# A GRU recurrence on one core: its loop written out, its gates in pair scans, its products placed anew

## The reference

```
hw = h @ gru_w_hh.T                     # 1024 -> 3 x 1024
xr, xz, xn = split(x_t @ gru_w_ih.T);  hr, hz, hn = split(hw)
r = sigmoid(xr + hr);  z = sigmoid(xz + hz)
n = tanh(xn + r * hn)
h = (1 - z) * n + z * h                 # kept for every token
```

## Time and profile before

| | |
|---|---|
| time, median of 3 runs | 4406.64 us (4403.16 to 4421.09) |
| profiled execution, its own time | 4422.04 us |
| span, first to last instruction | 4420.3 us |
| instructions | 182,219 |
| TensorE matmuls busy | 3978.8 us (90%) |
| TensorE weight loads busy | 2508.8 us (57%) |
| VectorE busy | 3130.2 us (71%) |
| ScalarE busy | 1511.4 us (34%) |
| GpSimd busy | 176.5 us (4%) |
| mean granted TensorE clock | 0.961 of full speed |

### The profile page before, as it was taken

One profiled execution on the slowest core, in us unless ns is written; L12 is line 12 of the kernel. 1 busy time (PEld: TensorE's weight loads), 2 busy tenths in 40 slices (PEclk: granted clock), 3 DMA queues, 4 the chain that ended last, 5 costly groups with the idle time before them and its releaser, 6 DMA issues. The chain is left out here.

```text
span 4420.3 us, 182219 instructions
## 1 busy us (share of the span) xinstructions
PE 3978.8 (90%) x76826; PEld 2508.8 (57%) x76826; DVE 3130.2 (71%) x14963; ACT 1511.4 (34%) x5111; POOL 176.5 (4%) x399
## 2 busy tenths in 40 slices
PE   4999599999999999999999999999999999986999
PEld 3776455555555555555555555555555555553665
DVE  2678677777777777777777777777777777776555
ACT  1112333333333333333333333333333333332322
POOL 1211000000000000000000000000000000000000
PEclk6879799999999999999999999999999999997999
DMA  2011300000000000000000000000000000000000
GB/s 64 17 36 48 133 3 4 4 4 4 3 4 4 3 4 4 3 4 3 4 4 4 3 4 4 3 4 4 3 4 3 4 4 4 4 12 26 14 9 12
DMA packets 46569, 52.79 MB, mean 12 GB/s; under 512 B 11668, under 2 KB 39572, under 8 KB 45716
## 3 DMA queue, kind: packets, MB, share of 16 engines
q1 hardware_dynamic: 45716, 40.48, 2.9%
HBM read 36.28 MB, written 4.19 MB: 9 GB/s over the span
## 5 line engine op out<-in xcount | busy, mean ns | idle before, releaser
L882 PE MATMUL psum<-room,h_parts 128*32 128x384 f16 x65536 | 2873.3, 328 | 168.3 <-DVE h_parts L1001 121.8
L882 PEld LDWEIGHTS psum<-room,h_parts 128*32 128x32 f16 x65536 | 1684.9, 97 | 1217.2 <-DVE h_parts L1001 419.1
L965 DVE STREAM_TRANSPOSE turned<-psum 128x128 f32<-128x128 f32 x1024 | 320.9, 313 | 624.2 <-PE psum L882 624.2
L1056 ACT ACTIVATE r_by<-gates 128x32 f32<-128x32 f32 x1024 | 252.9, 247 | 1297.5 <-DVE gates L947 1297.5
L747 DVE CUSTOM_DVE_ANT_0 products<-routes 128x128 f32<-128x128 f32 x1855 | 477.7, 270 | 4.4 <-ACT routes L740 3.0
L994 DVE TENSOR_TENSOR_SCAN state<-w_by,state 128x96 f32<-128x96 f32 x1024 | 366.6, 358 | 160.6 <-issue 93.2
L1065 ACT ACTIVATE state<-state 128x32 f32<-128x32 f32 x1024 | 256.4, 250 | 464.3 <-DVE state L994 464.3
L984 DVE TENSOR_TENSOR_SCAN pre_n<-r_by,n_terms 128x96 f32<-128x96 f32 x1024 | 366.6, 358 | 48.1
L890 PE MATMUL psum<-w_ih_s,x_now 128*32 128x256 f16 x6152 | 310.0, 279 | 85.3 <-issue 79.5
L947 DVE TENSOR_TENSOR gates<-turned 128x32 f32<-128x32 f32 x2048 | 360.7, 176 | 0.0
L976 DVE STREAM_TRANSPOSE n_terms<-psum 128x128 f32<-128x128 f32 x1024 | 331.6, 324 | 0.0
(11 more groups left out here) (157 smaller groups left out, 2699.3 us busy)
## 6 DMA issues: line engine op xcount, KB each, us to landing
xs_room<-in_L_ffn_gru_w_hh_dram SPq DMA_DIRECT2D x16, 1536.0 KB, 6.2
room<-in_L_attn_x_dram SPq DMA_DIRECT2D x8, 256.0 KB, 5.3
x_scratch<-room SPq DMA_DIRECT2D x8, 256.0 KB, 2.3
room<-x_scratch SPq DMA_DIRECT2D x32, 64.0 KB, 2.3
out_dram<-room SPq DMA_DIRECT2D x32, 64.0 KB, 2.0
xs_room<-in_L_ffn_gru_w_ih_dram SPq DMA_DIRECT2D x3, 512.0 KB, 5.3
xs_room<-in_L_ffn_gate_w_dram SPq DMA_DIRECT2D x2, 512.0 KB, 4.4
xs_room<-in_L_ffn_up_w_dram SPq DMA_DIRECT2D x2, 512.0 KB, 4.1
```

Of the source, the lines that this page charges most:

```text
L882: last = nc.tensor.matmul(psum[32 * j:32 * j + 32, half, 0:3 * P], h_parts[:, q, c, :], w_hh_s[:, s, half, 4 * c + j, :, :].rearrange("p g ...
L965: nc.vector.transpose(turned[:, half, 0, :], psum[:, half, 0:P]).then_inc(r_turned[half], 1)
```

## The change

The loop over tiles becomes a Python loop, so that all 512 steps stand in the program. Scans go over pairs in place of triples: the n part is transposed to `turned` and summed by an instruction of its own; z's sigmoid is taken as it is, VectorE multiplies it by the old state and makes the weights from it with a tensor_scalar, and the negated state is gone. The r transpose of half 1 keeps its place. All dots go behind half 1. Half 1's products take bank 1 and 3 by turns, and their token products are made one step earlier, ahead of the wait for h. Expr products are made one in every even step, the first of a tile in step 4; GpSimd's tile copy moves from step 0 to step 2. The two expr products that fall past the last step are made in the next block.

```
-        state = sb("state", [P, 2, CH * B, 3])
-        turned = sb("turned", [P, 2, 2, P])
+        state = sb("state", [P, 2, CH * B, 2])
+        turned = sb("turned", [P, 2, 3, P])
...
-            EXPR_FROM = 4
-            def over_tiles(eng, step):
-                with eng.Fori(0, NT) as n:
+            EXPR_FROM = 2
+            def bank_of(k, half):
+                return 0 if half == 0 else (1, 3)[k // 2 % 2]
+            def over_tiles(step):
+                for n in range(NT):
                     for k in range(SP_T):
                         step(n, k)
...
-                    if k == 0:
+                    if k == 2:
                         pool.wait_ge(expr_ps, n + 1)
                         nc.gpsimd.tensor_copy(x_tile[:, :], xn2T[:, bass.ds(n * P, P)]).then_inc(tile_staged, 1)
...
                 token_n()
+                token_share(0, 1)
...
                     if q == 0:
                         pe.wait_ge(bank_free[0], t1)
-                        token_share(0)
+                        token_share(k, 0).then_inc(x_used, 1)
+                        e = k // 2 - EXPR_FROM
+                        if e == 0:
+                            pe.wait_ge(tile_staged, n + 1)
+                            pe.wait_ge(expr_read, n + 1)
+                        last = expr_products(e % NEXP)
+                        if e == -1:
+                            last.then_inc(expr_ps, 1)
                     else:
...
                         token_n()
+                        token_share(k + 1, 1)
                     pe.wait_ge(h_ready[0], t1)
-                    state_share(q, 0, range(0, HALF))
+                    state_share(k, 0, range(0, HALF))
                     pe.wait_ge(bank_free[1], t1)
-                    if q == 0:
-                        token_share(1).then_inc(x_used, 1)
-                    state_share(q, 1, range(0, EARLY))
+                    state_share(k, 1, range(0, EARLY))
...
-                    if EXPR_FROM <= k < EXPR_FROM + NEXP:
-                        e = k - EXPR_FROM
...
+                def to_candidate(t1, k, half):
+                    nc.vector.transpose(turned[:, half, 1, :], gate_bank(k, half, 1)).then_inc(z_turned[half], 1)
                     dve.wait_ge(r_turned[half], t1)
-                    summed(q, half, 0).then_inc(r_in[half], 1)
-                    nc.vector.transpose(n_terms[:, :, here, 0:2].rearrange("p q k s -> p k q s"), bank[:, 2, :]).then_inc(bank_free[half], 1)
+                    summed(q, half, 0, gates[:, half, 0, :]).then_inc(r_in[half], 1)
+                    nc.vector.transpose(turned[:, half, 2, :], gate_bank(k, half, 2)).then_inc(bank_free[half], 1)
                     dve.wait_ge(z_turned[half], t1)
-                    summed(q, half, 1).then_inc(z_in[half], 1)
+                    summed(q, half, 1, gates[:, half, 1, :]).then_inc(z_in[half], 1)
+                    dve.wait_ge(bank_free[half], t1 + 1)
+                    summed(q, half, 2, n_terms[:, q, here, 0]).then_inc(n_in[half], 1)
                     dve.wait_ge(r_done[half], t1)
-                    dve.wait_ge(bank_free[half], t1 + 1)
+                    dve.wait_ge(n_in[half], t1)
                     nc.vector.tensor_tensor_scan(row(pre_n[:, half, :, :]), ...
-                def to_state(t1, q, half):
+                def to_state(t1, k, half):
+                    dve.wait_ge(z_done[half], t1)
+                    nc.vector.tensor_tensor(n_and_kept[:, half, :, 1], z_act[:, half, :], state[:, q, here, 1],
+                                            ALU.mult).then_inc(h_weighted[half], 1)
+                    nc.vector.tensor_scalar(w_by[:, half, :, 1], z_act[:, half, :], neg_h_scale[:, 0:1], h_scale_f[:, 0:1],
+                                            ALU.mult, ALU.add).then_inc(w_done[half], 1)
                     dve.wait_ge(n_done[half], t1)
+                    dve.wait_ge(h_weighted[half], t1)
                     dve.wait_ge(w_done[half], t1)
-                    dve.wait_ge(negated[half], t1)
-                    nc.vector.tensor_tensor_scan(row(state[:, 1 - q, here, :]), row(w_by[:, half, :, :]), row(state[:, q, here, :]),
+                    nc.vector.tensor_tensor_scan(row(state[:, 1 - q, here, :]), row(w_by[:, half, :, :]), row(n_and_kept[:, half, :, :]),
                                                  0.0, ALU.mult, ALU.add).then_inc(new_state[half], 1)
...
+                    turn_r(t1, k, 0)
+                    to_candidate(t1, k, 0)
+                    to_state(t1, k, 0)
+                    dve.wait_ge(kept, t1)
+                    to_high(t1, k, 0)
+                    turn_r(t1, k, 1)
+                    to_low(t1, k, 0)
+                    to_candidate(t1, k, 1)
+                    to_state(t1, k, 1)
+                    to_high(t1, k, 1)
+                    to_low(t1, k, 1)
...
                     if q == 0:
-                        dot(e, 3)
-                        dot(e, 4)
+                        for i in range(1, NSHIFT):
+                            dot(e, i)
                     else:
                         turn_xn(n * PAIRS + k // 2 + 2)
-                        last = dot(e, 0)
+                        dot(e, 0)
+                        sum_xn(n * PAIRS + k // 2 + 2)
+                        dot(e, NSHIFT)
+                        last = dot(e, NSHIFT + 1)
                         if k == 1:
                             last.then_inc(dots_done, 1)
...
-                        nc.scalar.activation(w_by[:, half, :, 2], gates[:, half, 1, :], ACT.Sigmoid,
-                                             scale=by_neg_unscale).then_inc(w_done[half], 1)
+                        nc.scalar.activation(z_act[:, half, :], gates[:, half, 1, :], ACT.Sigmoid,
+                                             scale=by_unscale).then_inc(z_done[half], 1)
...
-                        act.wait_ge(new_state[half], t1)
-                        nc.scalar.mul(state[:, 1 - q, here, 1], state[:, 1 - q, here, 2], -1.0).then_inc(negated[half], 1)
```

More of the change, by code:

```diff
@@ L809, in _ @@
                 nc.vector.tensor_scalar(first_h, first_h, h_scale_f[:, 0:1], None, ALU.mult)
[L810 to L811 removed]
+                nc.vector.tensor_scalar(neg_h_scale[:, :], h_scale_f, -1.0, None, ALU.mult)
                 dve.drain()
[L813 to L814 removed]
                 nc.vector.tensor_copy(part(h_parts[:, 0, :, :], 0), full)
@@ L931, in step, with summed, row @@
                         state_products(pe).then_inc(tile_ps, 1)
-                    if EXPR_FROM <= k < EXPR_FROM + NEXP:
-                        e = k - EXPR_FROM
-                        if e == 0:
-                            pe.wait_ge(tile_staged, n + 1)
-                            pe.wait_ge(expr_read, n + 1)
-                        last = expr_products(e)
-                        if e == NEXP - 1:
-                            last.then_inc(expr_ps, 1)
-                over_tiles(pe, step)
+                over_tiles(step)
             @block.vector
             def _(dve):
-                def summed(q, half, g):
+                def summed(q, half, g, dst):
                     by_part = turned[:, half, g, :].rearrange("p (k f) -> p k f", f=4)
-                    return nc.vector.tensor_tensor(gates[:, half, g, :], by_part[:, :, 2 * q], by_part[:, :, 2 * q + 1], ALU.add)
-                def row(triples):
-                    return triples.rearrange("p k three -> p (k three)")
+                    return nc.vector.tensor_tensor(dst, by_part[:, :, 2 * q], by_part[:, :, 2 * q + 1], ALU.add)
+                def row(pairs):
+                    return pairs.rearrange("p k two -> p (k two)")
                 def turn_xn(pairs):
@@ L964, in turn_r @@
+                def turn_r(t1, k, half):
                     dve.wait_ge(gates_ps[half], t1)
-                    nc.vector.transpose(turned[:, half, 0, :], psum[:, half, 0:P]).then_inc(r_turned[half], 1)
-                def to_gates(t1, q, half):
-                    bank = psum[:, half, 0:3 * P].rearrange("p (g r) -> p g r", g=3)
+                    nc.vector.transpose(turned[:, half, 0, :], gate_bank(k, half, 0)).then_inc(r_turned[half], 1)
+                def to_candidate(t1, k, half):
+                    q = k % 2
@@ L988, in to_state @@
                     here = slice(half * HB, (half + 1) * HB)
-                    parts = h_parts[:, 1 - q, half * HALF:(half + 1) * HALF, :]
-                    full = by_chunk(state[:, 1 - q, here, 2])
+                    dve.wait_ge(z_done[half], t1)
[3 more added lines that the diff above has]
+                                            ALU.mult, ALU.add).then_inc(w_done[half], 1)
@@ L1003, in step, with parts_of, full_of @@
+                def parts_of(q, half):
+                    return h_parts[:, 1 - q, half * HALF:(half + 1) * HALF, :]
+                def full_of(q, half):
+                    return by_chunk(state[:, 1 - q, half * HB:(half + 1) * HB, 1])
                 def step(n, k):
@@ L1039, in _ @@
```

(2 more changed lines are left out.)

90 lines of the change are left out of this document (38 added, 52 removed).

## The result

The changed kernel takes 4515.15 us (median of 4 runs, 4500.97 to 4520.60) against 4409.01 us before (median of 4): the ratio is 1.0232, with a 95% interval of 1.020 to 1.0264. It is 106 us slower. The forecast was 4280 us, faster.

A forecast was written before the change was run, and what follows sets the result against it. VectorE's chain was taken to bound the step, TensorE right behind. Loop -96, steps -51 (511 x -0.10) and two worse steps +20 made -127 us, from the median 4406.6 to 4280 us; range 4215 to 4360.

The forecast's parts named there:

- The loop: Loop over tiles written out: TensorE's issue waits at all 31 tile edges go, -96 us, bounds 0 and 99.8.
- the rival of a straight program that stalls: The jump gives nothing, since a straight program this long stalls in its fetching elsewhere: 4376 us, chance 0.05.
- Scans of pairs: VectorE's four scans a step go from 96 elements to 64, about 287 ns each: -0.28 us a step.
- The n sum: New VectorE sum between n transpose and candidate's scan: +0.13 us in half 1, +0.08 in half 0, +0.21 a step.
- The weights: VectorE's multiply by h and weights, where the dots were under tanh, just fit: 0, bounds 0 and +0.10 each half.
- the slower case: In tanh's shadow in half 1, added instructions run whole lengths one after another: 4551 us, half of it 4441; chance 0.07.
- VectorE's chain: VectorE's work through both halves of a step: shorter scans and added sums together give -0.07 us a step.
- TensorE's side: Half 1's token products made a step earlier give even steps back 0.06 us: -0.03 us a step on the mean.
- The two worse steps of a tile: Steps 0 and 1: TensorE late behind the state products, +0.35 us, and r 0.3 us late: +20 us, bounds 0 and 35.

The follow-up runs named there:

- e1: The kernel before with its loop over tiles written out and nothing else changed: 4280.9 us.
- e6: The changed kernel, same operations and order, one semaphore wait ahead of each scan and the wait for the kept states ahead of the step: 4343.2 us.
- e5: The changed kernel with only the wait for the kept states moved, from between half 0's state scan and fp16 copy to ahead of the step: 4506.2 us.
- e7: e1 with the change's new order of TensorE and GpSimd alone; VectorE keeps its triples and its order: 4294.3 us.
- e9: e1 with one more wait, met long before, ahead of the remainder in each half, two a step: 4340.4 us.
- e4: The changed kernel with the weights made on ScalarE, between z's sigmoid and tanh, in place of VectorE's tensor_scalar: 4403.2 us.
- e2: The changed kernel with its loop over tiles put back as a hardware loop: 4609.1 us.

## Why the prediction was wrong

**The loop: the step held, its size was too small.** 96 us were taken, from the edges alone; 128 came in e1 and 94 in the changed kernel, to which the sum applies. The reason given and the reading of the earlier trace rows were right. The further 32 us in e1 weren't foreseen. The instruction queue moved 9.52 MB, less than in the earlier trace rows, and the rival of a straight program that stalls fell.

**Scans of pairs: held.** 292 ns were measured for 287 forecast.

**The n sum: this step failed.** It was priced at +0.21 us a step, and the candidate's scan came 0.23 us later in half 1 and 0.18 in half 0: +0.41. Two sizes were off. The sum takes 217 ns, not 0.17 to 0.18. It writes every second element, where the sums whose time I took write a whole row, but so does the multiply with its 0.17; why it is longer stays open. And I let the scan start 0.03 us behind the sum, the gap of an instruction with one wait, though the diff puts two waits there; 0.10 passed.

**The weights: this step failed.** "They just fit: 0" rested on 246 ns for a like instruction in the earlier trace rows; with two scalars read from memory it took 298. They ended after tanh, by 0.04 us, and three waits then followed the weights at 0.13 us. The interval from scan to scan should have become 0.07 us shorter and didn't. With one wait (e6) it is 0.62 to 0.63 us, the 0.07 shorter that were forecast: the lengths did just fit, and the waits were what failed. The text named this place as the slower case, but as lengths that don't overlap, and there it was wrong: multiply and weights do overlap, starting 0.09 us apart.

**The kept wait: left out.** I let the copy follow its scan as before and didn't see that the diff moves a wait in between. It costs 0.07 us there (0.10 for 0.03), where it had cost 0.05 ahead of the state's scan; e5 gained only 0.024 a step since at its new place it adds 0.07 or 0.03 to the return.

**What the sum missed is the price of a wait.** I counted instructions and took waits that are met as free. VectorE's chain was forecast 0.07 us shorter and became 0.36 longer, in the middle of all normal steps; with one wait each (e6) it is 4.80 us, 0.41 less, and the kernel before has 4.84. The step is then 6.500 us; by the waits alone the change is 0.364 longer.

**TensorE's side: -0.03 failed, harmlessly**, by e7: 1.66 and 1.60 us were read as the price of the token products, but the normal steps stay at 6.37 and 6.44 without them. The transpose behind the longer return is the one with a second wait, for the xn sum. **The two worse steps of a tile, +20: nothing here.** With h of half 1 later, TensorE's lateness behind the state products is hidden. The two steps take 6.80 and 6.95 us, 0.09 over two normal ones, where the kernel before has 0.15; in e7, where the chain is short, the lateness shows (0.22 us). ScalarE's r sigmoid of step 2 is late by 0.10 us, not 0.3, and the candidate's scan waits for the sum until later than that.

**The range and the chances.** The slower rival was priced from 4441 to 4551 and decided at +0.15 us a step; 4515 lies there, though not for the rival's reason: lengths do overlap, waits are what was added. Its chance of 0.07 was too small because every gap on VectorE's chain was taken at 0.03 us, in all of the cases alike: sums, weights and waits went wrong together, not one by one.

## What to carry to other kernels

Where one engine's chain of short instructions bounds a recurrence, count the waits ahead of each as well as the instructions: a second one, met long before, cost 0.07 us and a third 0.03 more. Let several producers count up one semaphore. Moving a met wait to where the engine idles saved next to nothing here (e5), since it stood ahead of another wait there too. Whether it costs less behind the wait that is met last is worth a run. Write out a hot loop for itself, apart from a rewriting of its body: here one gave 128 us and the other took 234.

## What the runs showed of the hardware

A VectorE instruction behind one wait, for its own engine's last result, started 0.03 to 0.04 us after that result's end; behind two 0.10; behind three 0.13 (e6, e9, the changed kernel). The r transpose, which waits for TensorE while VectorE sits idle, comes 1.59, 1.66 and 1.69 us behind the remainder with one, two and three waits. When the first of three waits is the one for ScalarE's tanh and is met last, the scan starts 0.03 to 0.04 us after tanh's end (e4). No view shows the sequencer at these waits. The Trainium skill ("VectorE: DVE Perf Modes", The DRAIN you can't avoid) says that a semaphore after each instruction costs nothing extra. Here an instruction with no wait starts 0.08 us before the end of the one in front (the weights at 2006.99, the multiply's end at 2007.07), and one that waits for that one's result 0.03 after it, so the first wait isn't free in these runs, and further ones add to it.

At the jump back to the head of this loop TensorE sat idle 2.6 us (80.1 us in 31 waits); written out it cost nothing, and steps of the kernel before became 0.06 us shorter besides, those of the changed kernel not (e2). A tensor_scalar of 32 elements took 298 ns with two scalars per partition, and ScalarE's activation with scale and bias per partition 0.41 to 0.42 us, where plain sigmoids of the same size take 0.23.
